# Five rows' weighted sums moved from VectorE to ScalarE and TensorE in a recommender kernel

## The chip, the cores and the metric

The kernel runs on one core of a Trainium2 chip. The metric is the device time of one execution in microseconds (us). TensorE is called PE here, VectorE DVE, ScalarE ACT, GpSimd POOL and SyncE SP, as the profile has them.

## The reference

For each of 512 users there are 200 history rows of 128 numbers, a mask, an age and a popularity per row. The output is one normalised row of 128 numbers per user:

```python
mean_hist = (hist_items * maskf[..., None]).sum(1) / (maskf.sum(1) + 1e-06)
q = mean_hist @ Wq.T
scores = einsum('bd,btd->bt', q, hist_items @ Wk.T) * scale + log(decay + 1e-12)
attn = softmax(where(mask, scores, -inf))
long_term = einsum('bt,btd->bd', attn, hist_items @ Wv.T)
# short_term: mean of up to five rows, those at positions cnt-5 .. cnt-1 (cnt = number of masked rows)
g = sigmoid([mean_pop, mean_rec] @ gate_w.T + gate_b)
user = g * short_term + (1 - g) * long_term
out = (user - mean(user)) / sqrt(var(user) + 1e-05) * ln_gamma + ln_beta
```

The change concerns `g * short_term`, a weighted sum of five rows for each user, and the place of the last three lines.

## The kernel before, in words

A **tile** is 16 users: 128 partitions, 8 for each user, with 25 rows of 128 fp32 numbers in each (1600 KB). There are 32 tiles (0 to 31), two to a pair, and eight tiles (128 users) to a **group**; there are four groups. The output is made group by group.

Every engine has its own program, written out by hand; waits on semaphores tie them together, and each engine takes its instructions strictly in order. PE, ACT and POOL run over **slots** n = 0, 1, 2 ...; slot n is where tile n comes in. With n = 8g + i, `g` and `i` are the group and the place in it. DVE runs over **steps** s = 4g + k of a pair each; step s works on tile 2s-1 and then on tile 2s.

In slot n (for n over 7):

- SP has queued the load of tile n into one of ten buffers; it waits until the tile ten before it has been used up.
- PE makes the masked sums of tile n (`sum_rows`, L457, 25 matmuls), every fourth slot folds earlier results (L508), in slots with i = 7 turns them (L518), makes the attention-weighted sums of tile n-6 (`sum_row_pairs`, L465 and L469, 13 matmuls), the query of tile n-1 (`make_query`, L490) and the mean of tile n (L481). In slots with i = 7 `make_long` (L557) follows, the product of a group's attention sums with Wv, g being one more than that group's number counted from 0.
- ACT copies the weighted sums of tile n-7 (L645) and the mean of tile n-1 (L651), sums the last four of the eight products rows of tile n-3 (`sum_products`, L626, a copy with an accumulator), in odd slots takes two exponentials (L671), copies the masked sums of tile n (L636, with a scale from a tensor), sums the first four products rows of tile n-2 (L626), and copies the query of tile n-1 (L660).
- POOL builds two blocks of weights (`pblk` L345, `mblk` L334) in turns, and multiplies eight rows of tile n-1 by its query (`products`, L357). In a slot with i = 6 it issues the gather of a group's five rows a user into `taken` (L403); at i = 0 `inverse_deviation` (L364).
- DVE takes the dot products of the other 17 rows of each tile with the query, one instruction a row (`dots`, L969; tile 31 has 21), and mixes the rest of its work between them: five steps for the maxima of each pair (`user_maxima`), and a group's finish.

A group's **finish** on DVE is: five weighted rows summed into `short` (`short_term`, L886 and L889, between the dots of tile 8g+3), `finish_scales` in tile 8g+4, then in tile 8g+6 `finish_user` (L988, which waits for `make_long`), `finish_stats`, `finish_moments`, `finish_variance` and `finish_centre` (L1007); `finish_scale` (L1013) is in tile 8g+7. The last group is finished after the last tile's dots. What a slot's work on ACT, PE and POOL waits for is in the functions below.

## Time and profile before

| | |
|---|---|
| device time, median of 3 runs | 175.87 us (175.72 to 178.6) |
| profiled execution | 176.9 us, its span 175.1 us |
| mean granted PE clock | 0.985 |
| busy: PE / DVE / ACT / POOL | 147.1 / 153.0 / 122.2 / 143.8 us |
| DMA, mean over the span | 317 GB/s |

The span runs from the first to the last instruction; the device time has 1.8 us around it. Busy is the time in which an engine worked on an instruction. Instructions of one engine can overlap, and for PE the ends are modelled, so starts are the surer reading. In rows of the timeline the first number is the start in us from the span's start, the second the duration in us; in brackets stands idle time of the engine before it, and what ended it.

### The profile page before, as it was taken

What the parts mean: (1) busy time and instruction counts of PE and PEld (TensorE: products, weight loads), DVE (VectorE), ACT (ScalarE), POOL (GpSimd) and SP (SyncE); (2) the same over time, 40 slices, a digit from 0 to 9 for tenths busy, and PEclk for the clock granted to TensorE, in tenths of its full rate; (3) what the DMA queues carried; (4) which work ended last, traced back from release to release, by engine and by line L of the source; (5) the groups of instructions that cost most, each with busy time, mean ns of one, the idle gap of its engine ahead of it and who ended that gap; (6) DMA issues with size and microseconds to landing.
All of it is one profiled execution on the core that took longest, in us unless ns stands there. A gap on an engine that the chain in (4) does not pass through costs nothing. (4 is left out here: it accounts for less than half of the span.)

```text
span 175.1 us, 8178 instructions
## 1 busy us (share of the span) xinstructions
PE 147.1 (84%) x2811; PEld 113.6 (65%) x2811; DVE 153.0 (87%) x1289; ACT 122.2 (70%) x714; POOL 143.8 (82%) x110
## 2 busy tenths in 40 slices
PE   5766558777679999999998998999998999696780
PEld 5745446666465777877776775877785887364550
DVE  4589849797387899999999999999999999999843
ACT  2021657775385989897988889887889898877420
POOL 5748869889996998999999999999999996975101
PEclk9999996999999999999999999999999999999997
DMA  4799999999999989999999999999999940200000
GB/s 102 269 414 416 253 411 405 406 398 405 416 429 412 362 324 393 408 428 430 407 413 422 416 398 407 413 400 399 415 427 409 371 168 9 50 32 0 19 0 15
DMA packets 8008, 55.48 MB, mean 317 GB/s; under 512 B 2080, under 2 KB 3360, under 8 KB 4000
## 3 DMA queue, kind: packets, MB, share of 16 engines
q1 hardware_dynamic: 7152, 53.59, 77.2%
q0 software_dynamic: 576, 1.33, 2.3%
q8 instruction: 22, 0.36, 0.8%
q14 instruction: 18, 0.15, 0.2%
q10 hardware_dynamic: 240, 0.05, 0.2%
HBM read 54.70 MB, written 0.26 MB: 314 GB/s over the span
## 5 line engine op out<-in xcount | busy, mean ns | idle before, releaser
L969 DVE SCALAR_TENSOR_TENSOR junk_v<-x,ps_query 128x128 f32<-128x128 f32 x548 | 122.0, 279 | 9.6 <-ACT query L660 9.5
L626 ACT ACTIVATE gprod<-gprod 128x128 f32<-128x128 f32 x252 | 74.4, 302 | 11.7 <-POOL gprod L357 11.4
L357 POOL TENSOR_TENSOR gprod<-x,query 128x1024 f32<-128x1024 f32 (+1 forms) x32 | 75.0, 2343 | 8.5 <-ACT query L660 6.0
L457 PE MATMUL ps_acc<-x,mblk 128*16 128x128 f32 x1600 | 56.7, 278 | 6.7 <-DMA x<-in_r_hist_items_dram 6.1
L465 PE MATMUL ps_acc<-x,pblk 128*32 128x256 f32 x768 | 51.6, 381 | 7.9 <-POOL pblk L345 4.8
L457 PEld LDWEIGHTS ps_acc<-x,mblk 128*16 128x16 f32 x1600 | 45.9, 98 | 10.2 <-issue 7.3
L626 ACT ACTIVATION_READ_ACCUMULATOR gprod<-gprod 128x1 f32 x252 | 48.6, 193 | 0.0
L969 DVE DVE_READ_ACCUMULATOR junk_v<-x,ps_query 128x1 f32 x548 | 45.0, 82 | 0.0
L465 PEld LDWEIGHTS ps_acc<-x,pblk 128*32 128x32 f32 x768 | 27.0, 109 | 20.9 <-issue 5.6
L345 POOL TENSOR_TENSOR pblk<-own,ex 128x800 f32<-128x800 f32 (+1 forms) x17 | 24.3, 1432 | 3.8 <-ACT ex L671 3.7
L334 POOL TENSOR_TENSOR mblk<-own,mask_f 128x800 f32<-128x800 f32 (+1 forms) x17 | 25.0, 1471 | 0.2
L636 ACT ACTIVATE sums<-ps_acc,rcnt_rows 128x128 f32<-128x128 f32 x32 | 11.4, 357 | 10.4 <-PE ps_acc L457 10.4
L490 PE MATMUL ps_query<-wqk,mean_p 128*128 128x128 f32 x64 | 15.6, 326 | 2.6 <-ACT mean_p L651 2.6
L490 PEld LDWEIGHTS ps_query<-wqk,mean_p 128*128 128x128 f32 x64 | 9.5, 188 | 9.0 <-issue 5.7
L645 ACT ACTIVATE wx<-ps_acc 128x256 f32<-128x256 f32 x32 | 11.6, 369 | 4.7 <-PE ps_acc L469 3.1
L481 PEld LDWEIGHTS ps_acc<-fold_z,sums 128*128 128x128 f32 x64 | 9.6, 190 | 7.7 <-ACT sums L636 6.6
L481 PE MATMUL ps_acc<-fold_z,sums 128*128 128x16 f32 x64 | 11.0, 248 | 4.0 <-ACT sums L636 3.7
L476 PE MATMUL ps_group<-own_rows 128*128 128x128 f32 x74 | 11.5, 314 | 1.8 <-POOL own_rows L370 1.8
L651 ACT ACTIVATE mean_p<-ps_acc 128x128 f32<-128x128 f32 x32 | 8.8, 274 | 5.2 <-PE ps_acc L481 5.2
L469 PE MATMUL ps_acc<-x,pblk 128*16 128x128 f32 x64 | 12.2, 273 | 0.0
L671 ACT ACTIVATE ex<-kept,nmax_p 128x25 f32<-128x25 f32 x32 | 9.8, 311 | 3.3 <-DVE nmax_p L934 3.3
L476 PEld LDWEIGHTS ps_group<-own_rows 128*128 128x128 f32 x74 | 10.8, 229 | 1.8 <-POOL own_rows L370 1.8
(117 smaller groups left out, 134.0 us busy)
## 6 DMA issues: line engine op xcount, KB each, us to landing
x<-in_r_hist_items_dram SPq DMA_DIRECT2D x31, 1600.0 KB, 10.3
x<-in_r_hist_items_dram SPq DMA_DIRECT2D x1, 832.0 KB, 7.9
x<-in_r_hist_items_dram SPq DMA_DIRECT2D x1, 768.0 KB, 6.3
decay_s<-in_r_hist_age_hours_dram SPq DMA_DIRECT2D x4, 100.0 KB, 13.8
out_dram<-y SPq DMA_DIRECT2D x4, 64.0 KB, 5.0
mask_u<-in_r_hist_mask_dram SPq DMA_DIRECT2D x1, 100.0 KB, 7.1
wq<-in_L_rec_Wq_dram SPq DMA_DIRECT2D x1, 64.0 KB, 7.3
wk<-in_L_rec_Wk_dram SPq DMA_DIRECT2D x1, 64.0 KB, 7.4
```

The lines of the kernel that those rows point to most:

```text
L334: nc.gpsimd.tensor_tensor(mblk[:, s % 2, t:t + tiles, :, :].rearrange("p t r u -> p (t r) u"), own[:, :].unsqueeze(1).broadcast_to([P, til ...
L345: nc.gpsimd.tensor_tensor(pblk[:, s % 2, t:t + tiles, :, :].rearrange("p t r u -> p (t r) u"), own[:, :].unsqueeze(1).broadcast_to([P, til ...
L357: nc.gpsimd.tensor_tensor(gprod[:, t, 0:k * D].rearrange("p (r d) -> p r d", d=D), rows(at(s, t), ROWS - k, ROWS), query[:, s % 2, t, :].u ...
L457: ins = nc.tensor.matmul(dst[c:c + TU, 0:D], blk[:, s % 2, t, m, :], x[:, at(s, t), m * D:(m + 1) * D], start=(m < CG), stop=(m >= ROWS - CG))
L465: nc.tensor.matmul(dst[c:c + 2 * TU, 0:2 * D], blk[:, s % 2, t, m:m + 2, :].rearrange("p r u -> p (r u)"), x[:, at(s, t), m * D:(m + 2) * ...
L469: return nc.tensor.matmul(dst[c:c + TU, 0:D], blk[:, s % 2, t, m, :], x[:, at(s, t), m * D:(m + 1) * D], start=False, stop=True)
L476: nc.tensor.matmul(dst, turned, turned, start=True, stop=True)
L481: nc.tensor.matmul(mean_cols(s, t), sums[:, t, :], fold, start=True, stop=True).then_inc(mean_done, 1)
L490: nc.tensor.matmul(c_query[t], mean_p[:, t, :, :].rearrange("p u c -> p (u c)"), wqk[:, :], start=True, stop=True).then_inc(query_done, 1)
L626: ins = nc.scalar.activation(src, src, ACT.Copy, accum_out=score[:, s % 2, t, at_row:at_row + 1])
L645: nc.scalar.activation(wx[:, s % 2, t, :], wx_bank(s, t)[:, 0:2 * D], ACT.Copy).then_inc(wx_copied, 1)
L969: ins = V.scalar_tensor_tensor(out=junk_v[:, t, r, :], in0=x[:, at(s, t), r * D:(r + 1) * D], scalar=1.0, in1=c_query[t], op0=ALU.mult, op ...
```

## The change

`short_term` goes. ACT now multiplies each gathered row in place by its weight (`scale_taken`: two rows in slots with i = 4, two with i = 5, one with i = 6, and all five of the last group in slot 32). PE adds the five by matmuls with the identity matrix (`make_short`, five matmuls of 128x128, in slots with i = 7 and in slot 33), and ACT copies the sum to `short` (`copy_short`, in slots with i = 0 and in slot 34). `taken` gets two buffers. `make_long` goes from the slot with i = 7 to the next one (the last group's stays), and waits for `copy_short`. DVE's `finish_user` to `finish_variance` go from rows 2 to 5 of tile 8g+6 to rows 11 to 14 of it, `finish_centre` from row 14 of that tile to row 1 of the next, and `finish_scale` from row 1 of that next tile to row 14. `inverse_deviation` goes behind the products in POOL's slot. Of the six matmuls that `keep_busy` issues before the weighted sums of tile 28, two are left.

```diff
+TAKEN_PARTS = {4: (0, 2), 5: (2, 4), 6: (4, LAST)}
-BUSY_FIRST, BUSY_LEAD, BUSY_LAST = 13, 4, {NTILE - 4: 6}
+BUSY_FIRST, BUSY_LEAD, BUSY_LAST = 13, 4, {NTILE - 4: 2}
...
-        taken = sb("taken", [P, LAST, D])
+        taken = sb("taken", [P, 2, LAST, D])
...
             def gather(g):
-                if has(g, 1):
-                    pool.wait_ge(short_part, g * LAST)
+                if has(g, 2):
+                    pool.wait_ge(short_done, g - 1)
...
+            def make_short(q):
+
+                pe.wait_ge(taken_scaled, (q + 1) * LAST)
+                if has(q, 1):
+                    pe.wait_ge(user_ready, q)
+                for i in range(LAST):
+                    ins = nc.tensor.matmul(short_v, ident[:, :], taken[:, q % 2, i, :], start=(i == 0), stop=(i == LAST - 1))
+                ins.then_inc(short_done, 1)
+
             def make_long(g):
+                pe.wait_ge(short_copied, g)
+                pe.wait_ge(rden_ready, g)
                 pe.wait_ge(att_t_ready, g)
-                pe.wait_ge(rden_ready, g)
...
+                if n == NTILE + 1:
+                    make_short(NGROUP - 1)
                 if w == LAST_TILE:
                     sum_weights(g)
...
-                if i == 7 and 0 < g:
+                if i == 0 and 1 < g <= NGROUP:
+                    make_long(g - 1)
+                if i == 7 and 0 < g < NGROUP:
+                    pe.wait_ge(rden_ready, g)
+                    make_short(g - 1)
+                if n == NTILE + 7:
                     make_long(g)
...
+            def scale_taken(q, a, b):
+
+                if a == 0:
+                    act.wait_ge(gathered, q * 16 + 16)
+                    act.wait_ge(gate_ready, 1)
+                for i in range(a, b):
+                    row = taken[:, q % 2, i, :]
+                    nc.scalar.activation(row, row, ACT.Copy, scale=lw[:, bass.ds(q, 1), i]).then_inc(taken_scaled, 1)
+
+            def copy_short(q):
+
+                act.wait_ge(short_done, q + 1)
+                if has(q, 1):
+                    act.wait_ge(user_ready, q)
+                nc.scalar.activation(short[:, :], short_v, ACT.Copy).then_inc(short_copied, 1)
...
+                if n > SLOTS_OF_GROUP and n % SLOTS_OF_GROUP == 0 and n <= NTILE:
+                    copy_short(n // SLOTS_OF_GROUP - 2)
...
+                g, i = divmod(n, SLOTS_OF_GROUP)
+                if 0 < g < NGROUP and i in TAKEN_PARTS:
+                    scale_taken(g - 1, *TAKEN_PARTS[i])
+                if n == NTILE:
+                    scale_taken(NGROUP - 1, 0, LAST)
                 if n == NTILE + 1:
                     copy_weighted(w + 1)
...
-                    if i == (1 if g < NGROUP else DOTS - 3) and k == 0 and has(g, 2, NGROUP):
+                    if i == 1 and k == 0 and has(g, 2, NGROUP):
+                        finish_centre(g - 1)
+                    if i == (DOTS - 3 if g < NGROUP else DOTS_LAST - 2) and k == 0 and has(g, 2, NGROUP):
                         finish_scale(g - 1)
...
-                    if 2 < i < 3 + LAST and k == 2 and fin and has(s, 0):
-                        short_term(g - 1, i - 3)
...
-                    parts = {2: finish_user, 3: finish_stats, 4: finish_moments, 5: finish_variance, 14: finish_centre}
+                    parts = {11: finish_user, 12: finish_stats, 13: finish_moments, 14: finish_variance}
                     if g == NGROUP:
-                        parts[15] = finish_scale
+                        parts.update({15: finish_centre, 16: finish_scale})
```

PE, slots 23 and 24 (the second group's), before: L490 is the query, L481 the mean, L557 `make_long`, L457 the masked sums, L465 and L469 the weighted sums.

```order
L490 MATMUL ps_query<-wqk,mean_p 128x128
L481 MATMUL ps_acc<-fold_z,sums 128x16
L557 MATMUL ps_fin<-wv_t,att_t 128x128
L457 MATMUL ps_acc<-x,mblk 16x128 x25
L465 MATMUL ps_acc<-x,pblk 32x256 x12
L469 MATMUL ps_acc<-x,pblk 16x128
L490 MATMUL ps_query<-wqk,mean_p 128x128
L481 MATMUL ps_acc<-fold_z,sums 128x16
L457 MATMUL ps_acc<-x,mblk 16x128 x25
```

The same place now (every line number is one higher up to L491; L562 is `make_short`, L570 `make_long`):

```order
L491 MATMUL ps_query<-wqk,mean_p 128x128
L482 MATMUL ps_acc<-fold_z,sums 128x16
L562 MATMUL ps_fin<-taken,ident 128x128 x5
L458 MATMUL ps_acc<-x,mblk 16x128 x25
L466 MATMUL ps_acc<-x,pblk 32x256 x12
L470 MATMUL ps_acc<-x,pblk 16x128
L491 MATMUL ps_query<-wqk,mean_p 128x128
L482 MATMUL ps_acc<-fold_z,sums 128x16
L570 MATMUL ps_fin<-wv_t,att_t 128x128
L458 MATMUL ps_acc<-x,mblk 16x128 x25
```

Five matmuls stand where `make_long` stood, and `make_long` stands one slot, that is 40 other matmuls, later.

ACT, slot 21 (i = 5), before: four products rows of tile 18, two exponentials, the masked sums of tile 21, four products rows of tile 19, the query of tile 20.

```order
L626 ACTIVATE gprod,score<-gprod 128x128 x4
L671 ACTIVATE ex,wsum<-kept,nmax_p 128x25 x2
L636 ACTIVATE sums<-ps_acc,rcnt_rows 128x128
L626 ACTIVATE gprod,score<-gprod 128x128 x4
L660 ACTIVATE query<-ps_query 128x128
```

Now:

```order
L646 ACTIVATE gprod,score<-gprod 128x128 x4
L691 ACTIVATE ex,wsum<-kept,nmax_p 128x25 x2
L656 ACTIVATE sums<-ps_acc,rcnt_rows 128x128
L710 ACTIVATE taken<-taken,lw 128x128 x2
L646 ACTIVATE gprod,score<-gprod 128x128 x4
L680 ACTIVATE query<-ps_query 128x128
```

Two scaled copies of gathered rows stand ahead of the products rows and of the query.

DVE, the second half of tile 22 (its rows 9 to 16) and the first rows of tile 23, now; L1001 is a dot, L1019 `finish_user`, L1024 to L1033 the three steps behind it, L1038 `finish_centre`, L966 the last of the five steps for a pair's maxima:

```order
L1001 SCALAR_TENSOR_TENSOR junk_v,score<-x,ps_query 128x128
L1019 SCALAR_TENSOR_TENSOR ps_dve<-ps_fin,long_scale,short 128x128
L1001 SCALAR_TENSOR_TENSOR junk_v,score<-x,ps_query 128x128
L953 STREAM_TRANSPOSE pmax_t<-pmax 128x32
L1024 BN_STATS bn<-ps_dve 128x6
...
L1033 TENSOR_SCALAR vare<-mv 128x1
L1001 SCALAR_TENSOR_TENSOR junk_v,score<-x,ps_query 128x128 x2
L966 STREAM_TRANSPOSE nmax_p<-numax 128x32
L1001 SCALAR_TENSOR_TENSOR junk_v,score<-x,ps_query 128x128 x2
L1038 SCALAR_TENSOR_TENSOR ps_dve<-ps_dve,mv,gam 128x128
```

`finish_user` stood behind two dots of this tile; now eleven dots and two of the maxima's steps are ahead of it.

## Rows read from the trace of the kernel before

**Rows 1.** Busy time of each engine in a stretch; last PE clock, DMA share, GB/s.
```profile
110.00:120.00 10.00, 10.00 (x232) 8.17 (x235) 9.96 (x97) 8.80 (x56) 9.56 (x7) 1.00 1.00 401
```

**Rows 2.** Timeline of DVE, tile 27: two of the five rows' steps, a dot between.
```profile
142.22 0.35 DVE L889 SCALAR_TENSOR_TENSOR ps_dve<-taken,lw,ps_dve 128x128 f32<-128x128 f32 x1
142.48 0.28 DVE L969 SCALAR_TENSOR_TENSOR junk_v<-x,ps_query 128x128 f32<-128x128 f32 x1
...
142.68 0.35 DVE L889 SCALAR_TENSOR_TENSOR ps_dve<-taken,lw,ps_dve 128x128 f32<-128x128 f32 x1
```

**Rows 3.** Timeline of POOL, products of tiles 20 to 23.
```profile
110.38 2.38 POOL L357 TENSOR_TENSOR gprod<-x,query 128x1024 f32<-128x1024 f32 x1
...
114.37 2.37 POOL L357 TENSOR_TENSOR gprod<-x,query 128x1024 f32<-128x1024 f32 x1
116.91 1.02 POOL L403 DMA_INDIRECT taken<-in_r_hist_items_dram,first_row  x1 [0.17 <-issue]
...
119.47 2.40 POOL L357 TENSOR_TENSOR gprod<-x,query 128x1024 f32<-128x1024 f32 x1
...
124.05 2.36 POOL L357 TENSOR_TENSOR gprod<-x,query 128x1024 f32<-128x1024 f32 x1
```

**Rows 4.** Timeline of ACT, slots 21 and 22.
```profile
108.37 0.35 ACT L636 ACTIVATE sums<-ps_acc,rcnt_rows 128x128 f32<-128x128 f32 x1
108.83 0.31 ACT L626 ACTIVATE gprod<-gprod 128x128 f32<-128x128 f32 x1
...
112.86 0.31 ACT L626 ACTIVATE gprod<-gprod 128x128 f32<-128x128 f32 x1 [0.70 <-POOL gprod L357]
...
114.04 0.25 ACT L660 ACTIVATE query<-ps_query 128x128 f32<-128x128 f32 x1
```

**Rows 5.** Groups of instructions of ACT and PE by form: busy us, mean ns.
```profile
L636 ACT ACTIVATE sums<-ps_acc,rcnt_rows 128x128 f32<-128x128 f32 x32 | 11.4, 357 | 10.4 <-PE ps_acc L457 10.4
L660 ACT ACTIVATE query<-ps_query 128x128 f32<-128x128 f32 x32 | 8.4, 261 | 4.0 <-PE ps_query L490 4.0
...
L476 PE MATMUL ps_acc<-own_rows 128*128 128x128 f32 x12 | 1.6, 284 | 0.0
```

**Rows 6.** Timeline of PE: queries of tiles 17 and 23, `make_long` between them.
```profile
97.51 0.49 PE L490 MATMUL ps_query<-wqk,mean_p 128*128 128x128 f32 x2
...
118.31 0.47 PE L557 MATMUL ps_fin<-wv_t,att_t 128*128 128x128 f32 x2
...
121.85 0.49 PE L490 MATMUL ps_query<-wqk,mean_p 128*128 128x128 f32 x2
```

**Rows 7.** Timeline of ACT, the copy of tile 17's query.
```profile
98.04 0.28 ACT L660 ACTIVATE query<-ps_query 128x128 f32<-128x128 f32 x1
```

**Rows 8.** Timeline of DVE: tile 22's `finish_user` and row 11, tile 23's first row.
```profile
120.57 0.35 DVE L988 SCALAR_TENSOR_TENSOR ps_dve<-ps_fin,long_scale,short 128x128 f32<-128x128 f32 x1
...
123.30 0.28 DVE L969 SCALAR_TENSOR_TENSOR junk_v<-x,ps_query 128x128 f32<-128x128 f32 x1
...
125.08 0.29 DVE L969 SCALAR_TENSOR_TENSOR junk_v<-x,ps_query 128x128 f32<-128x128 f32 x1
```

**Rows 9.** Timeline, the end: PE's and ACT's slot 32, tile 31's first dot.
```profile
154.88 0.49 PE L490 MATMUL ps_query<-wqk,mean_p 128*128 128x128 f32 x2
...
155.55 0.31 ACT L626 ACTIVATE gprod<-gprod 128x128 f32<-128x128 f32 x1 [1.29 <-POOL gprod L357]
...
156.73 0.25 ACT L660 ACTIVATE query<-ps_query 128x128 f32<-128x128 f32 x1
...
158.75 0.28 DVE L969 SCALAR_TENSOR_TENSOR junk_v<-x,ps_query 128x128 f32<-128x128 f32 x1
...
166.32 1.50 PE L465 MATMUL ps_acc<-x,pblk 128*32 128x256 f32 x24 [1.07 <-DVE pblk L954]
```

**Rows 10.** The last gather alone (its line, 148 to 156 us).
```profile
L403 POOL DMA_INDIRECT taken<-in_r_hist_items_dram,first_row x1: 1022/1022/1022, 150.5 to 150.5; - x1
...
DMA to landing us min/median/max: 3.8/3.8/3.8
```

More of the change, by code:

```diff
@@ L164, in build @@
         hide_v, at = ps_dve[:, 0:GROUP_ROWS], GROUP_ROWS
-        short_v, user_v = ps_dve[:, at:at + D], ps_dve[:, at + D:at + 2 * D]
+        user_v, short_v = ps_dve[:, at + D:at + 2 * D], ps_fin[:, 384:384 + D]
         own_v, rden_v = ps_dve[:, at + 2 * D:at + 2 * D + TU], ps_dve[:, at + 2 * D + TU:at + 2 * D + TU + 1]
@@ L185, in build @@
         gate_in, gate_exp, gate_ready, rows_ready = sem("gate_in"), sem("gate_exp"), sem("gate_ready"), sem("rows_ready")
-        short_part = sem("short_part")
+        taken_scaled, short_done, short_copied = sem("taken_scaled"), sem("short_done"), sem("short_copied")
         gathered = sem("gathered")
@@ L399, in gather @@
             def gather(g):
[L401 to L402 removed]
+                if has(g, 2):
+                    pool.wait_ge(short_done, g - 1)
                 nc.gpsimd.indirect_dma_start(
[L404 removed]
+                    out=taken[:, g % 2, :, :].rearrange("p i d -> p (i d)"), out_offset=None, in_=items_rows,
                     in_offset=bass.IndirectOffsetOnAxis(ap=first_row[:, g:g + 1], axis=0)).then_inc(gathered, 16)
@@ L413, in slot @@
                     build_pblk(w)
-                if i == 0 and has(g, 2, NGROUP):
-                    inverse_deviation(g - 2)
                 if tile(n + 2) and n % PAIR == 0:
@@ L426, in slot @@
                     build_pblk(FIRST_LONE + 1, 1)
+                if i == 0 and has(g, 2, NGROUP):
+                    inverse_deviation(g - 2)
                 if n < NGROUP:
@@ L547, in sum_weights @@
                 pe.wait_ge(wsum_ready, g)
+                if g == NGROUP:
+                    pe.wait_ge(short_copied, g)
                 if g == 1:
@@ L723, in slot @@
                 if n == NTILE + 2:
+                    copy_short(NGROUP - 1)
                     sum_products(LAST_TILE, 0, ROWS - DOTS_LAST)
@@ L879, in setup_last_weights @@
                 dve.wait_ge(gate_ready, 1)
-            def short_term(g, i):
-                w = lw[:, bass.ds(g, 1), i]
-                if i == 0:
-                    dve.wait_ge(gathered, g * 16 + 16)
-                    ins = V.tensor_scalar(short_v, taken[:, i, :], w, None, ALU.mult)
-                else:
-                    dve.wait_ge(short_part, g * LAST + i)
-                    ins = V.scalar_tensor_tensor(out=short_v if i < LAST - 1 else short[:, :], in0=taken[:, i, :], scalar=w,
-                                                 in1=short_v, op0=ALU.mult, op1=ALU.add)
-                ins.then_inc(short_part, 1)
             def group_hide(g):
@@ L1053, in step @@
                                 last_block()
-                                for j in range(LAST):
-                                    if j == LAST - 2:
-                                        lay_out_sums(s + 1)
-                                    short_term(g - 1, j)
+                                lay_out_sums(s + 1)
                     if i in parts:
```

3 lines of the change are left out of this document (1 added, 2 removed).

## The prediction

> **What bounds the kernel now.** I read the windows first, then the timeline of each engine in one group of slots, then the end. The window shows DVE at 9.96 of 10 us, PE at 10.00, POOL at 9.56, ACT at 8.80 and the DMA share at 1.00 [rows 1]. Five things are near full, so the busiest cannot be named from shares; the reader has to look for who waits for whom.
>
> POOL's products give the pace. Those of tile 20 start at 110.38 and those of tile 21 at 114.37, 3.99 us later; the next two starts, with a gather and the reciprocal root between them, are at 119.47 and 124.05 [rows 3]. The 3.99 is a loop: products of 2.38, after which ACT, idle for them [0.70 at 112.86], sums four rows and copies the next query at 114.04, for 0.25, and POOL starts at 114.37 [rows 3, 4]. DVE has no part in this loop. From tile 21 to 22 POOL alone sets the time: its gather starts at 116.91 and the weights' block follows it up to 119.47 [rows 3].
>
> DVE is full, but it runs behind the queries: tile 31's query is ready at 156.73 + 0.25 = 156.98, and its first dot is at 158.75, 1.77 us later [rows 9]. So a shorter DVE programme first eats that backlog, and then DVE waits for queries. At the very end DVE does set the time: PE waits for DVE's last block until 166.32 [rows 9], and all that follows hangs on it. What counts is thus when tile 31's dots begin, and how many steps lie among them.
>
> **The change, part by part.** The sum is for tile 31's first dot and what is behind it.
>
> Removed: five steps a group on DVE. One step starts at 142.22, a dot at 142.48, the next step at 142.68: a step takes 0.26 and a dot 0.20 of DVE's time [rows 2]. Three groups have theirs in the full stretch: 15 x 0.26 = 3.9 us. The last group's five come after the last dots, beside PE's last weighted sums and ahead of nothing that ends late; I cost them at nothing. They can at most give 1.3 if that cover were not there.
>
> Added on ACT: a row's scaled copy. The trace has no such copy from SBUF with a scale from a tensor. The plain copy from PSUM takes 261 ns, the one with such a scale 357 ns [rows 5], so 0.10 is the scale; a products row takes 0.31 from SBUF [rows 4]. A lone copy would be some 0.40, and neighbours overlap; I take 0.30 a row, with ends at 0.20 and 0.40. In slots with i = 4 and 6 ACT has 0.70 idle before the products rows, as at 112.86 [rows 4], which covers two copies or one. With i = 5 it hasn't: in slot 21 the masked sums end at 108.37 + 0.35 = 108.72 and the products row starts at 108.83 [rows 4], 0.11 of room for 0.60. These copies stand in the loop, ahead of the query, so 0.49 goes into the pace, once a group (slots 13, 21, 29): 3 x 0.49 = 1.5 us (0.9 to 2.1). In slot 32 all five stand before products rows that start at 155.55 after 1.29 idle [rows 9]: 1.5 - 1.29 = 0.2 (0 to 0.7). They wait for the last gather too, issued at 150.5 and landed 3.8 later, at 154.3 [rows 10], just when that idle time begins (154.26); if it came 1 us later, the query of tile 31 would, and what hides it is only that the loads have ended by then. `copy_short` has the 0.25 of a query's copy [rows 4] and lies in slots whose idle time covers it; if not, 0.25 a group.
>
> Added on PE: `make_short`. Six matmuls of 128x128 in a row take 1.6 us [rows 5], so five take 1.33 and are 1.33 late for all that PE does after them: masked sums, weighted sums, queries. What hides that is PE's lead over ACT. It isn't everywhere: PE's query of tile 17 ends at 97.51 + 0.49 = 98.00, ACT copies it at 98.04 [rows 6, 7], a lead of 0.04. ACT's own delay of 0.49 covers a part. Ends: nothing (the lead elsewhere is larger and PE catches up) and 1.33 - 0.49 = 0.84 in each of three groups. I take 0.1 a group, 0.3 in all, nearer to the low end, since the end of the stretch has room: PE's last `make_short` in a busy slot stands before weighted sums that wait for POOL.
>
> The new wait on DVE: `finish_user`, now in row 11 of tile 8g+6, waits for `make_long`, now a slot later and behind `make_short`. In the second group the query before it starts at 121.85 [rows 6]; with 1.33 added and `make_long`'s own share (its 0.47 [rows 6], 0.4 of it between neighbours) gone, that is 122.8; it takes 0.49, `make_long` 0.47: done at 123.75. DVE's row 11 began at 123.30 with four steps of the finish ahead of it [rows 8], which now stand behind it. At some 0.15 each (0 to 0.26) that is 122.7, and with the 1.3 saved 121.4. So DVE waits 1.0 to 2.3 us, and all dots behind it and the pair's maxima wait too, which ACT's exponentials need. From row 11 to the next tile are 125.08 - 123.30 = 1.78 [rows 8], plus 0.6 for the four steps, less 0.2 for `finish_centre`, moved on: 2.2. Tile 23 starts at 125.95 and not 125.08: the saved 1.3 is gone, and 0.9 more. It is DVE's backlog that takes this up, since the next group saves another 1.3 before its own wait.
>
> At the end the same: PE's query of tile 31 ends at 154.88 + 0.49 [rows 9], `make_long` at 155.85, row 11 of tile 30 then, and tile 31 starts 2.2 later at 158.05, not 158.75: a gain of 0.7, whatever DVE saved earlier. Of the moves, `finish_centre` is now among tile 31's dots: 0.25 back. `inverse_deviation` stays in POOL's queue, behind one products instruction, and the sum of POOL's work is the same: nothing. A `gather` waits for `short_done` of two groups before, long done: nothing.
>
> `keep_busy` loses four matmuls in the gap before tile 28's weighted sums, and `make_short` puts five into it: nothing, at a granted clock of 1.00 [rows 1]. If the clock did fall there, a weighted sum of 1.50 [rows 9] would take up to 1.5 more.
>
> **Sum.** Delay of the queries: 1.5 + 0.2 + 0.3 = 2.0. Gain at tile 31: 0.7 - 0.25 = 0.45. Net 1.5 us later. The profiled execution took 176.9 us with a span of 175.1, so 178.4; it was 1.03 above the median of 175.87, so the median is forecast at 177.4. The range of this case by the bounds: 176.0 to 179.3.
>
> **Rivals.** *A, the backlog goes and little else.* The copies overlap better than I think or slot 21 has more room, and `make_long` comes in time for DVE. Then tile 31 starts when its query is ready: 1.77 earlier [rows 9], less 0.25 for `finish_centre`: 1.5 faster, 174.4. For it speaks that ACT idles in two slots of three; against it the 0.11 us in slot 21 and the 121.85 of PE's query.
>
> *B, PE is the pacemaker.* PE shows 10.00 of 10 us busy [rows 1] and a lead of 0.04 at tile 17. If it has no time to catch up, each group adds the full 1.33 of `make_short`: 4.0, + 0.2 - 0.45 = 3.75 us, 179.6. It decides from the point where PE's lead over ACT stays under 1.33 through a whole group. Against it: PE's ends are modelled, so its busy share is too high.
>
> *C, the fullest engine sets the time.* If DVE bounds the stretch, as 9.96 of 10 suggests, all 3.9 us come back: 172.0. Against it is the lag of the dots behind the queries, which DVE cannot make shorter for POOL. The Trainium skill (Perfetto Trace Analysis, Identifying the Most-Contended Engine) says that the engine with the highest occupancy is the one to relieve first, and by that rule this rival would be the forecast; the lag of 1.77 us speaks against it here.
>
> **Chances.** Forecast 0.56, A 0.26, B 0.13, C 0.05. A measurement of this kernel tells about 2%, 3.5 us, from no change: faster by over that is C alone, 0.05; slower by over that (from 179.4) is most of B and the forecast's upper end, 0.12; within it 0.83. The range holds 8 in 10: it takes in the forecast, most of A (down to 174.0) and the nearer half of B (179.9).
>
> **What would show each step.** ACT: the products row of slot 21 starts some 0.5 late after the two scaled copies, each with a duration near 0.40; the idle time in slots 20 and 22 shrinks by 0.6 and 0.3. DVE: before `finish_user` in tiles 14, 22 and 30 a wait of 1 to 2 us that ends with `make_long`; DVE's share falls below 9.7 of 10. POOL: products of tile 8g+5 half a microsecond later in each group, so that eight tiles take over 34 us. PE: five matmuls in 1.3 us. Tile 31's first dot near 160.0. I am wrong if the scaled copies are hidden (A), if PE's queries come later than ACT is free (B), or if the last gather lands late enough to hold ACT in slot 32.

## The result and the profile after

| | before | changed |
|---|---|---|
| device time, median of 4 runs | 175.84 us (175.72 to 178.6) | 180.24 us (179.7 to 180.71) |
| profiled execution, its span | 176.9, 175.1 us | 179.7, 178.0 us |
| mean granted PE clock in it | 0.985 | 0.978 |

The medians lie 4.4 us apart. The ratio, which takes only executions within 1.5% of a kernel's fastest, is 1.0225 with a 95% interval of 1.0175 to 1.0276: 3.1 to 4.8 us slower, and whether by more than 2% isn't settled. The forecast was 177.4, and its range ended at 179.9. By the ratio the change stands at 175.87 x 1.0225 = 179.8, just inside; its own median, 180.24, is just outside. The direction was right and the size too small.

The profiled executions lie only 2.8 us apart, and 0.7 of that is there before any of the moved work runs. So I read one stretch: from tile 10's first dot to the start of the last `y`, the kernel's last computation. Its rows on DVE in the changed kernel (start, duration) are tile 10's first dot, tile 31's first dot and the last `y`:

```profile
70.44 0.29 DVE L1001 SCALAR_TENSOR_TENSOR junk_v<-x,ps_query 128x128 f32<-128x128 f32 x1
...
161.26 0.28 DVE L1001 SCALAR_TENSOR_TENSOR junk_v<-x,ps_query 128x128 f32<-128x128 f32 x1
...
175.66 0.35 DVE L1044 SCALAR_TENSOR_TENSOR y<-ps_dve,rstd,bet 128x128 f32<-128x128 f32 x1 [0.40 <-POOL rstd L365]
```

The same of before; its dot between is in [rows 9]:

```profile
69.75 0.29 DVE L969 SCALAR_TENSOR_TENSOR junk_v<-x,ps_query 128x128 f32<-128x128 f32 x1
...
172.81 0.35 DVE L1013 SCALAR_TENSOR_TENSOR y<-ps_dve,rstd,bet 128x128 f32<-128x128 f32 x1 [0.40 <-POOL rstd L364]
```

Before takes 172.81 - 69.75 = 103.06 us, 89.00 of it up to tile 31's first dot. The changed kernel takes 175.66 - 70.44 = 105.22, with 90.82 up to that dot: 2.16 us more. The rest of the 2.8, 0.69, lies ahead of tile 10.

What the forecast named is in the profile. ACT, slots 21 and 22, where [rows 4] had the masked sums, a pause of 0.11 and the products row:

```profile
111.03 0.35 ACT L656 ACTIVATE sums<-ps_acc,rcnt_rows 128x128 f32<-128x128 f32 x1
111.28 0.69 ACT L710 ACTIVATE taken<-taken,lw 128x128 f32<-128x128 f32 x2
111.87 0.30 ACT L646 ACTIVATE gprod<-gprod 128x128 f32<-128x128 f32 x1
...
113.03 0.27 ACT L680 ACTIVATE query<-ps_query 128x128 f32<-128x128 f32 x1
```

Two copies take 0.59 from the first one's start to the products row's, so 0.30 each, as taken. ACT in slot 32 has the last group's five, and it waited 0.49 for the last gather there, the risk that the forecast named. Then DVE's waits from 80 to 172 us (total, times, longest):

```profile
157.72 1.57 ACT L710 ACTIVATE taken<-taken,lw 128x128 f32<-128x128 f32 x5 [0.49 <-DMA taken<-in_r_hist_items_dram,first_row]
```
```profile
DVE ps_dve L1019 <- PE ps_fin L570: 4.8, 3, 2.2
```

`finish_user` now waits for `make_long` three times, 2.22, 1.83 and 0.77 us, as the forecast had it for the first two (1.0 to 2.3). Less of DVE's time is busy too: 9.60 of 10 us from 110 to 120, 8.02 from 120 to 130.

These waits give an account of the stretch from DVE's side. In the kernel before DVE waits for nothing between the first dots of tiles 10 and 31, so those 89.00 us are the length of its own programme. The changed one is 3.9 us of steps shorter, has `finish_centre` (0.25) more, and waits 4.8 for `make_long` and 0.4 for a query: 89.00 - 3.65 + 5.2 = 90.55, and 90.82 was measured. At the end the chain is the forecast's, one matmul behind the other (PE, then DVE):

```profile
158.36 0.49 PE L491 MATMUL ps_query<-wqk,mean_p 128*128 128x128 f32 x2
158.68 0.39 PE L570 MATMUL ps_fin<-wv_t,att_t 128*128 128x128 f32 x2
```
```profile
159.11 0.36 DVE L1019 SCALAR_TENSOR_TENSOR ps_dve<-ps_fin,long_scale,short 128x128 f32<-128x128 f32 x1 [0.77 <-PE ps_fin L570]
```

Tile 31's first dot comes 2.15 us after this `finish_user` (forecast 2.2). So what has to be explained is why PE's query of tile 31 is late: it starts 87.92 us after tile 10's first dot, and 85.13 before [rows 9], 2.8 later. A place where it enters is on PE and on what follows it, slots 17 and 18 (PE, ACT, POOL):

```profile
98.41 0.38 PE L509 MATMUL ps_group<-wx,fold_odd_z 128*32 128x128 f32 x2 [1.94 <-issue]
...
100.14 0.49 PE L491 MATMUL ps_query<-wqk,mean_p 128*128 128x128 f32 x2
```
```profile
100.66 0.28 ACT L680 ACTIVATE query<-ps_query 128x128 f32<-128x128 f32 x1 [1.49 <-PE ps_query L491]
```
```profile
101.02 2.39 POOL L358 TENSOR_TENSOR gprod<-x,query 128x1024 f32<-128x1024 f32 x1 [1.71 <-ACT query L680]
```

PE stands still for 1.94 us in the middle of the folds of weighted sums, on nothing that the profile names; then its query of tile 17 is late, ACT waits 1.49 for it and POOL 1.71. In the kernel before, the same place had a stall of its own, "[0.88 <-issue]" at 96.34, and PE's query came 0.04 ahead of ACT [rows 6, 7].

POOL's products need the queries, so their starts show where the queries become late. How much later they start than before, each kernel counted from its own tile 10, in us (negative is earlier; worked out from the starts of POOL's products):

| tile | 12 | 16 | 17 | 20 | 24 | 28 | 31 |
|---|---|---|---|---|---|---|---|
| before, again (e0) | 0.01 | 0.47 | 0.43 | 0.41 | 0.23 | 0.45 | 0.47 |
| changed | 0.49 | 0.38 | 1.93 | 2.30 | 2.15 | 2.76 | 2.95 |
| changed, again | 0.50 | 0.38 | 1.54 | 1.89 | 1.72 | 2.84 | 2.90 |
| e1, PE's part | 0.46 | 1.38 | 1.35 | 1.33 | 1.20 | 1.63 | 1.65 |
| e2, ACT's part | 1.37 | 1.64 | 1.81 | 2.20 | 2.04 | 2.43 | 2.74 |
| e3, DVE's relief | -0.01 | 0.17 | 0.44 | 0.46 | 0.49 | 1.04 | 1.06 |
| e9, fewer matmuls | 0.99 | 1.08 | 1.06 | 1.95 | 1.80 | 2.57 | 3.18 |
| e12, all moved | 0.70 | 0.84 | 0.81 | 0.87 | 0.75 | 0.82 | 0.83 |

The row of the unchanged kernel is the measure of noise here: up to 0.6 us (0.59 at tile 13), of which nothing reached DVE's dots, since they run at least 0.9 behind their queries. Tile 31's first dot came after 89.01 us in it, against 89.00. In the changed kernel three steps stand where ACT's copies do: 0.49 by tile 12, 0.34 at tile 20, 0.36 at tile 28. One step, 1.55 at tile 17 (1.16 in the second execution), stands behind the stall of PE.

### The profile page after: what moved, and what is told of

Its sections match the earlier page's. It is cut to its first block and busy times, and to the rows that moved or that the text cites. A ratio compares the mean times of both kernels' runs of the same rounds, so it can differ in the third digit from the quotient of the medians.

```text
span 178.0 us, 8258 instructions
## 1 busy us (share of the span) xinstructions
PE 149.9 (84%) x2843; PEld 117.4 (66%) x2843; DVE 148.2 (83%) x1269; ACT 128.4 (72%) x738; POOL 143.9 (81%) x110
## 3 DMA queue, kind: packets, MB, share of 16 engines
q0 software_dynamic: 576, 1.33, 2.2%
## 5 line engine op out<-in xcount | busy, mean ns | idle before, releaser
L1001 DVE SCALAR_TENSOR_TENSOR junk_v<-x,ps_query 128x128 f32<-128x128 f32 x548 | 121.1, 281 | 10.8 <-ACT query L680 10.5
L458 PE MATMUL ps_acc<-x,mblk 128*16 128x128 f32 x1600 | 58.1, 282 | 7.0 <-DMA x<-in_r_hist_items_dram 5.0
L458 PEld LDWEIGHTS ps_acc<-x,mblk 128*16 128x16 f32 x1600 | 46.7, 99 | 11.2 <-issue 7.5
L646 ACT ACTIVATION_READ_ACCUMULATOR gprod<-gprod 128x1 f32 x252 | 49.6, 197 | 0.0
L1001 DVE DVE_READ_ACCUMULATOR junk_v<-x,ps_query 128x1 f32 x548 | 45.7, 83 | 0.0
L466 PEld LDWEIGHTS ps_acc<-x,pblk 128*32 128x32 f32 x768 | 27.6, 109 | 17.2 <-issue 5.0
L491 PE MATMUL ps_query<-wqk,mean_p 128*128 128x128 f32 x64 | 15.6, 326 | 3.1 <-ACT mean_p L671 2.6
L491 PEld LDWEIGHTS ps_query<-wqk,mean_p 128*128 128x128 f32 x64 | 9.5, 188 | 9.2 <-issue 5.9
L680 ACT ACTIVATE query<-ps_query 128x128 f32<-128x128 f32 x32 | 8.5, 267 | 5.5 <-PE ps_query L491 5.5
```

Source lines behind the costliest of these rows:

```text
L458: ins = nc.tensor.matmul(dst[c:c + TU, 0:D], blk[:, s % 2, t, m, :], x[:, at(s, t), m * D:(m + 1) * D], start=(m < CG), stop=(m >= ROWS - CG))
L466: nc.tensor.matmul(dst[c:c + 2 * TU, 0:2 * D], blk[:, s % 2, t, m:m + 2, :].rearrange("p r u -> p (r u)"), x[:, at(s, t), m * D:(m + 2) * ...
L491: nc.tensor.matmul(c_query[t], mean_p[:, t, :, :].rearrange("p u c -> p (u c)"), wqk[:, :], start=True, stop=True).then_inc(query_done, 1)
L646: ins = nc.scalar.activation(src, src, ACT.Copy, accum_out=score[:, s % 2, t, at_row:at_row + 1])
L1001: ins = V.scalar_tensor_tensor(out=junk_v[:, t, r, :], in0=x[:, at(s, t), r * D:(r + 1) * D], scalar=1.0, in1=c_query[t], op0=ALU.mult, op ...
```

## The experiments

Whole times of the kernel before spread from 175.7 to 184.8 us over the chips that these runs fell on; in the profiled executions up to 5 us of that lie ahead of tile 10 (69.75 and 74.91). "Stretch" is always tile 10's first dot to the last `y`, "lag" is tile 31's first dot minus the end of ACT's copy of its query (1.77 before, 0.63 after). The stretch repeated to 0.1 us in the two executions of each of the two kernels. Each experiment's is from one execution, though, and the traces show that this isn't always enough: several differ from their kernel before their edit has had any effect. Where that is so, it is said.

**e0 and e7: both kernels once more,** unchanged, on another chip, the same for both.

> The kernel before, unchanged, for one profile beside the others of this chip. From the first dot of tile 10 to the first dot of tile 31 it took 89.0 us in the first profile (69.75 to 158.75); 88.7 to 89.6 is expected again, whatever the start of the execution costs.

> The changed kernel, unchanged, again beside the kernel before on one chip. It was 4.4 us slower (1.0225); the forecast had 1.5. If the forecast's terms are right and the rest was the chip's start, 1 to 2.5 us slower; if the full price is real, 3 to 5. From tile 10's first dot to tile 31's the first profile of it took 90.8 us.

The kernel before, execution of 182.05 us:

```profile
74.91 0.29 DVE L969 SCALAR_TENSOR_TENSOR junk_v<-x,ps_query 128x128 f32<-128x128 f32 x1
...
177.98 0.35 DVE L1013 SCALAR_TENSOR_TENSOR y<-ps_dve,rstd,bet 128x128 f32<-128x128 f32 x1 [0.39 <-POOL rstd L364]
```

The changed kernel, execution of 182.99 us:

```profile
73.69 0.29 DVE L1001 SCALAR_TENSOR_TENSOR junk_v<-x,ps_query 128x128 f32<-128x128 f32 x1
...
178.95 0.35 DVE L1044 SCALAR_TENSOR_TENSOR y<-ps_dve,rstd,bet 128x128 f32<-128x128 f32 x1 [0.40 <-POOL rstd L365]
```

103.07 and 105.26: the stretch's 2.2 us stand. Ahead of tile 10 the order has turned, 74.91 for the kernel before and 73.69 for the changed one, so the 0.69 of the first pair is within what executions differ by. The medians of this chip are 183.81 (6 runs) against 181.71 (11 runs), 2.1 apart; the fastest runs are further apart (181.87 against 176.93 and 177.27), so whole times leave the size open.

**e1: PE's part alone,** on the kernel before: five matmuls of 128x128 into an idle bank, read by nobody, at the end of slots 15 and 23, ahead of the masked sums of tiles 16 and 24.

```diff
+                if n > SLOTS_OF_GROUP and n % SLOTS_OF_GROUP == 0:
+                    keep_busy(sum_bank(s, t)[:, 3 * D:4 * D], LAST)
```

> The kernel before, with five matmuls of 128x128 added on PE where make_short now stands (slots 15, 23, 31, ahead of the next masked sums), and nothing else; they write an unused part of a bank, the output is the reference's. Theory ACT (the forecast: PE has lead enough to take most of it): 0 to 0.8 us slower. Theory PE (PE is the pacemaker, rival B): 1.33 us a group for two or three groups, 2.5 to 4 us slower.

Stretch 104.39, 1.3 longer, but this is not the price of the ten matmuls. The first of them starts at 92.34. Tile 13's products had started at 88.05, already 1.49 later than before, and tile 14's first dot came 1.04 later; PE had stopped on the way, among instructions that both kernels have:

```profile
84.90 0.50 PE L457 MATMUL ps_acc<-x,mblk 128*16 128x128 f32 x9 [1.14 <-issue]
```

Behind the added matmuls the products are no later: 1.49 at tile 14, 1.35 at tile 17, 1.20 at tile 24. At tiles 16 and 24, right behind them, the steps are 0.01 and 0.02. So here ten matmuls cost the queries nothing that can be seen, and rival B's 1.33 a group is not there. What five matmuls cost where PE's lead is 0.04, this run can't say, since it ran late anyway. The median was 181.74 against 182.44 (ratio 1.0066, 0.990 to 1.023): whole times can't resolve it.

**e2: ACT's part alone,** on the kernel before: the scaled copies go to a spare tile, from the identity matrix, in the changed kernel's slots.

```diff
+                for i in range(a, b):
+                    nc.scalar.activation(spare[:, i, :], ident[:, :], ACT.Copy, scale=lw[:, bass.ds(q, 1), i])
```

> The kernel before, with scaled copies added on ACT where scale_taken now stands (two in slots 8g+4, two in 8g+5, one in 8g+6, five in slot 32); they copy the identity matrix with a weight as scale into a spare tile, the output is the reference's. Theory ACT: 0.49 us a group, 1.5 us and up to 0.2 for slot 32, so 1.5 to 1.7 us slower. Theory PE (ACT has room, PE sets the pace): 0 to 0.5 us slower.

Stretch 105.06, 2.0 longer, median 181.87 (6 runs) against 182.44. Not all of it is the copies' either: PE, unchanged, stopped for 0.54 and 0.86 us in slots 12 and 14, and the products were 1.01 late at tile 11, where the changed kernel's were 0.13. The steps that stand at the copies are 0.36 at tile 12, 0.35 at tile 20, 0.38 at tile 28 and 0.31 at tile 31, 1.4 in all, and the same places and nearly the same sizes as in the changed kernel. This is what shows ACT's part. Since e1 and e2 each carry such a delay, their 1.3 and 2.0 can't be added or compared with the 2.2.

**e3: DVE's relief alone,** on the kernel before: of a group's five scaled rows it computes only the last.

```diff
-                if i == 0:
-                    ins = V.tensor_scalar(short_v, taken[:, i, :], w, None, ALU.mult)
-                else:
...
+                if i == LAST - 1:
+                    V.tensor_scalar(short[:, :], taken[:, i, :], w, None, ALU.mult).then_inc(short_part, 1)
```

> The kernel before, with one of the five steps of short_term on DVE left (the fifth row times its weight alone; the other four rows are left out of the output). It prices the relief of DVE: 4 x 0.26 = 1.04 us a group. Theory backlog (DVE runs behind the queries and its relief is worth at most the lag of tile 31's dots): 1.0 to 1.8 us faster. Rival C (the fullest engine bounds the stretch): 3.1 us faster. If relief is worth nothing: within 0.3.

Stretch 102.85, 0.2 us shorter (whole times 181.62 against 182.44, ratio 0.984, 0.976 to 0.993). The relief was smaller than planned, though. The step that was left now writes to SBUF at once, and instead of 0.26 it took 1.53, 0.28 and 0.92 us in the three groups. The long ones end with an instruction of POOL, at 81.58 and 81.50 the first time (DVE, then POOL):

```profile
80.05 1.53 DVE L886 TENSOR_SCALAR short<-taken,lw 128x128 f32<-128x128 f32 x1
```
```profile
79.95 1.55 POOL L345 TENSOR_TENSOR pblk<-own,ex 128x800 f32<-128x800 f32 x1
```

So DVE won some 1.4 us (3.9 less 2.5) and not 3.1. Its dots were 0.93 earlier at tile 22; then they waited for queries (0.7 us in all), which in this execution ran up to 1.06 later than before, behind stalls of PE. The lag fell from 1.77 to 0.24 and 0.46 was left at tile 31. DVE's own programme did set the time of the kernel before up to there, as its missing waits show; what its relief can win is bounded by how far its dots lie behind the queries, at least 0.93 and at most 2.4 us. The 3.9 of rival C aren't there to be had, but this run alone doesn't show it; e12 does.

**e4: `make_long` back in its slot,** on the changed kernel, so that DVE needn't wait for it.

```diff
-                if i == 0 and 1 < g <= NGROUP:
-                    make_long(g - 1)
                 if i == 7 and 0 < g < NGROUP:
-                    pe.wait_ge(rden_ready, g)
+                    make_long(g)
                     make_short(g - 1)
```

> The changed kernel, with make_long back in the slot with i = 7, ahead of make_short, and without its wait for copy_short (finish_user waits for copy_short instead). If the 1 to 2.3 us for which DVE waits at finish_user in tiles 14, 22 and 30 cost the end, this takes them away: 0.5 to 2 us faster than the changed kernel's 180.2, so 178.2 to 179.7. If PE or ACT set the pace, DVE's wait only eats its backlog: within 0.5 of the changed kernel.

DVE's waits for `make_long` are gone but for the one at the very end (the 4.8 us of the three full groups), and in their place it waits 6.0 us for queries. The stretch is 106.62, 1.4 longer than the changed kernel's. The products start 4.54 later at tile 31, 2.71 of it by tile 17. But tile 14's first dot, ahead of the first instruction that differs, was already 2.0 us later than in the changed kernel (PE had stopped for 1.14 us in slot 14), and from there on this run is 0.6 us shorter. The whole times point that way too: median 182.42 (8 runs) against 182.44 for the kernel before on that chip, ratio 0.989 (0.977 to 1.000), where the changed kernel's was 1.0225. Whether `make_long`'s old place wins something stays open.

**e6: one matmul where `make_short` has five,** on the changed kernel; the sum is the last row alone.

```diff
-                for i in range(LAST):
-                    ins = nc.tensor.matmul(short_v, ident[:, :], taken[:, q % 2, i, :], start=(i == 0), stop=(i == LAST - 1))
+                for i in range(LAST - 1, LAST):
+                    ins = nc.tensor.matmul(short_v, ident[:, :], taken[:, q % 2, i, :], start=True, stop=True)
```

> The changed kernel with one of make_short's five matmuls left (the fifth row's; the sum of the other four is left out of the output). Theory PE: 4 x 0.27 = 1.07 us a group come back, 2 to 3.2 us faster than the changed kernel. Theory ACT (the scaled copies in slots 13, 21 and 29 and DVE's wait are the price): within 0.8 of it, and faster mostly by what DVE waits less for make_long.

Less work on PE, and the stretch is 108.21, 3.0 longer (median 184.58, 6 runs, against 183.81 for the changed kernel and 181.71 for the kernel before on that chip). This is no effect of the edit in the main: `make_short` first runs at 91.8, and tile 14's first dot, ahead of it, was already 2.3 us later than in the changed kernel. What differs is PE's rows with idle time that no wait explains:

```profile
84.14 0.50 PE L458 MATMUL ps_acc<-x,mblk 128*16 128x128 f32 x9 [1.88 <-issue]
...
104.40 1.27 PE L466 MATMUL ps_acc<-x,pblk 128*32 128x256 f32 x17 [2.27 <-issue]
...
143.29 0.40 PE L458 MATMUL ps_acc<-x,mblk 128*16 128x128 f32 x4 [1.53 <-issue]
```

They stand in the middle of rows of equal matmuls, one after another from one tile. Taking every idle time of PE's weight loads over 0.42 us that no wait explains and that follows a transfer on the queue of instructions, there are 11.1 us of such stalls in the stretch, against 6.7 in the changed kernel and 3.3 before, 6.1 in e0. Each follows a transfer on the queue of instructions: one lands at 82.63, 103.02 and 141.83, and PE goes on 1.4 to 1.5 us later. In the changed kernel, from 96.05 to 97.1 us (packets, MB, share):

```profile
q8 instruction: 1, 0.02, 5.5%
```

That packet of 16 KB starts at 96.11 and takes 0.93; PE, stopped since 96.5, goes on at 98.41, 1.4 us after it landed. At the 21 such places in the stretches of four kernels (before, changed, e6, e8) the distance is 1.3 to 1.5.

The places are fixed by the count of instructions. Counting PE's weight loads from the start of the program, they come ahead of the 1101st, 1226th, 1351st, 1477th, 1603rd, 1728th, 1853rd, 1978th, 2103rd, 2229th, 2354th or 2480th, one off at most, in e0 and e1 too: 125 or 126 apart or a multiple of that, whatever stands there. Their length isn't fixed. Ahead of the 1101st, which stands ahead of what the edits change on PE in these kernels, the gap between two weight loads was 0.40 before, 1.21 in e0, 1.51 in e1, 0.31 in the changed kernel and 2.26 in e6. So a change that adds or removes matmuls moves work against these points, and how long PE stands at each differs from one execution to the next.

**e8: the changed kernel with its programme shifted** by sixteen one-column matmuls in slots 2 to 5, ahead of everything measured.

```diff
+                if 2 <= n <= 5:
+                    for _ in range(4):
+                        nc.tensor.matmul(ps_group[:, D:D + 1], ident[:, :], ones[:, :], start=True, stop=True)
```

> The changed kernel with 16 one-column matmuls added on PE in slots 2 to 5, where PE waits for loads: they cost nothing there, and shift by 64 instructions where the loads of PE's own instructions fall in the program. From tile 10's first dot to the last y the changed kernel took 105.2 and 105.3 us, with PE stalled in slot 18 for 2.2 to 2.3 us with nothing that it waited for. Theory supply (these stalls are PE waiting for instructions, and it is they that make PE late): the stalls move to other places and the stretch changes by 0.5 to 2 us, either way. Theory work (PE is late by make_short's 1.33 us a group alone): the stalls move and the stretch stays at 105.2 within 0.3.

```profile
111.53 0.85 PE L458 MATMUL ps_acc<-x,mblk 128*16 128x128 f32 x24 [1.14 <-issue]
...
117.73 1.27 PE L466 MATMUL ps_acc<-x,pblk 128*32 128x256 f32 x18 [0.99 <-issue]
```

The stall that ends at 111.53 belongs to the one transfer that took long, 107.58 + 2.50 = 110.08: again 1.45 after the landing, and not after the start. These two stand ahead of the 1728th and the 1854th weight load again, which is now work of 32 weight loads earlier. The stall in front of tile 17's query is gone, and so is the step there (0.65 late at tile 17, not 1.93), although `make_short` is as it was; other steps came at tiles 20 and 21 instead (1.53, then 2.28), and the stretch is 105.65 (median 183.34, 4 runs, against 180.65 for the kernel before on that chip). So the step at tile 17 needs the stall, and this shift won nothing by moving it.

**e9 and e10: both kernels with a quarter fewer matmuls.** The masked sums take two rows per matmul (128x256), and two matmuls of the mean fold them. PE's count of matmul instructions (two for each matmul of the program) falls from 2843 to 2139 in the changed kernel and from 2811 to 2107 in the kernel before, the transfers of instructions from 22 to 17.

```diff
-                sum_rows(sum_bank(s, t), mblk, s, t, 0, loaded).then_inc(sum_done, 1)
+                for a, part_loaded, count in loaded[:1]:
+                    pe.wait_ge(part_loaded, count)
+                sum_row_pairs(sum_bank(s, t), mblk, s, t, 0, loaded[1:]).then_inc(sum_done, 1)
```

> The changed kernel with the masked sums made like the weighted ones, by row pairs of 256 columns (13 matmuls in place of 25 a tile, one more matmul for each mean, ACT copies 256 columns and not 128; the output is the reference's). PE's busy time of a tile hardly changes (1.9 us for 1.7), its instructions of a slot fall by about a quarter. Theory supply: stalls without a wait nearly vanish, PE leads ACT everywhere but by its work, and the stretch from tile 10's first dot to the last y is 1 to 2 us shorter than 105.2. Theory work: 0.1 us a slot more on ACT and 0.2 on PE, so 1 to 3 us longer.

> The kernel before with the same row pairs for the masked sums (the output is the reference's). Its stretch from tile 10's first dot to the last y was 103.07 in two executions, with 3.7 and 6.5 us of such stalls, so PE has enough lead there. Theory supply and theory ACT agree: no gain in that stretch, 0 to 2 us longer for ACT's wider copy (0.1 us a slot) in the odd slots. A gain of over 0.5 would say that PE sets the pace before the change too.

In e9, PE's waits from 70 to 176 us name engines alone, the longest of them POOL, while the changed kernel's begin with two that name none (1.9 and 1.6 us):

```profile
PE ps_acc L469 <- POOL pblk L346: 1.6, 2, 1.1
```

Without a stall the stretches are 105.19 and 103.05, within 0.1 of the 105.22 and 103.06 with them (medians 181.29 and 180.97, 4 runs each, too few to tell 2 us in the whole time). So the stalls don't make the 2.2 us between the kernels: the change costs 2.1 in a pair that has none. This pair is the cleanest in the document. In e9 the step at tile 17 is gone (1.08 at 16, 1.06 at 17), and the steps at ACT's copies are larger, 0.99 at tile 12, 0.89 between tiles 17 and 20, 0.77 between 24 and 28; ACT's masked sums are wider here too, so how much of that is the copies alone isn't shown. Up to tile 31's first dot POOL waits 6.4 us for ACT's query in e9 and 2.0 in e10; ACT waits for no query of PE in e9. And DVE, which waits for nothing in e10 until then, has these waits in e9 from 70 to 162 us:

```profile
DVE ps_dve L1025 <- PE ps_fin L576: 4.7, 3, 2.3
DVE junk_v L1007 <- ACT query L686: 0.8, 2, 0.5
```

By DVE's account, 5.5 of waits less 3.65 of relief are 1.85, and tile 31's first dot is 1.80 later than in e10. So without stalls it is ACT that holds the queries up, and DVE loses by waiting more than it won by working less.

**e5: ACT's copies in even slots,** where it idles for POOL (i = 2, 4, 6), for two of the three groups.

```diff
+TAKEN_EVEN = {2: (0, 2), 4: (2, 4), 6: (4, LAST)}
...
-                if 0 < g < NGROUP and i in TAKEN_PARTS:
-                    scale_taken(g - 1, *TAKEN_PARTS[i])
+                parts = TAKEN_PARTS if g == 1 else TAKEN_EVEN
+                if 0 < g < NGROUP and i in parts:
+                    scale_taken(g - 1, *parts[i])
```

> The changed kernel with the scaled copies of the second and third group in slots with i = 2, 4 and 6, where ACT has idle time, and none in i = 5 (the first group's must stay). Theory ACT: 2 x 0.49 = 1.0 us faster than the changed kernel. Theory PE: within 0.3 of it.

The step between tiles 24 and 28 shrank from 0.61 to 0.43, and at tile 28 itself from 0.36 to 0.01, as the theory of ACT has it; yet at tile 20, with the first such group, it was 1.2 from tile 17, not 0.37, with a stall of PE of 2.25 us on the way (0.93 in the changed kernel). The stretch is 105.59, 0.4 worse than the changed kernel's, with stalls of 7.5; the median is 182.65 (6 runs), 1.2 better than the changed kernel's 183.81 on that chip. So the copies' price in slots with i = 5 went at tile 28, and what the whole gains stays open.

**e12: all of it at once:** e4's order, e5's slots, e9's pairs, and in slot 32 three copies before tile 31's query and two behind it.

```diff
-                    scale_taken(NGROUP - 1, 0, LAST)
+                    scale_taken(NGROUP - 1, 0, 3)
...
+                if n == NTILE:
+                    scale_taken(NGROUP - 1, 3, LAST)
```

> The changed kernel with every cost that the runs point to moved off: masked sums by row pairs (no PE stalls), make_long back in the slot with i = 7 (no wait on DVE in tiles 14, 22 and 30), the scaled copies of groups 2 and 3 in slots with i = 2, 4, 6, those of group 1 as two, one and two, and of the last group's five only three ahead of tile 31's query. If the relief of DVE is worth its 1.77 us of lag once nothing else is late: the stretch from tile 10's first dot to the last y is 101.6 to 102.6, against 103.07 of the kernel before. If ACT's copies and PE's five matmuls cost wherever they stand: 103.5 to 105.5. Rival C (DVE bounds): 99.5 to 100.5.

```profile
74.53 0.29 DVE L1008 SCALAR_TENSOR_TENSOR junk_v<-x,ps_query 128x128 f32<-128x128 f32 x1
...
162.81 0.29 DVE L1008 SCALAR_TENSOR_TENSOR junk_v<-x,ps_query 128x128 f32<-128x128 f32 x1
...
164.56 0.18 DVE L947 TENSOR_TENSOR kept<-score,ps_dve 128x25 f32<-128x25 f32 x1 [0.57 <-ACT gprod L650]
...
177.97 0.35 DVE L1052 SCALAR_TENSOR_TENSOR y<-ps_dve,rstd,bet 128x128 f32<-128x128 f32 x1 [0.40 <-POOL rstd L366]
```

Now the queries are only 0.83 late at tile 31 and the lag is 0.03: tile 31's dots begin after 88.28 us, 0.7 earlier than before. But all of DVE's relief, 3.65 us, has bought no more than that: it has caught up and waits for queries nine times, 2.4 us in all. This is what shows that rival C's 3.9 aren't to be had. From tile 31's first dot, 1.75 us later, it waits 0.57 for ACT's rows of an earlier tile. From that dot to the last `y` are 15.16 us, not 14.06. The stretch is 103.44: 1.8 better than the changed kernel, and no better than the kernel before (103.06). The whole times say more, 179.11 (6 runs) against 180.51 (11 runs), ratio 0.981 (0.974 to 0.989): faster, by 2% or not. That gain lies ahead of tile 10 or in what executions differ by, and no run here says which.

## Why the prediction was right or wrong

Its sum was a delay of the queries, less what tile 31's dots win on them, plus what is added behind. Each has its number, for the first profiled pair:

| term | forecast | measured |
|---|---|---|
| ACT's copies in three groups | 3 x 0.49 = 1.5 | 0.49 + 0.34 + 0.36 = 1.2 |
| slot 32 | 0.2 | 0.18 |
| PE's `make_short` | 0.3 | 1.55, at tile 17 (1.16 in e7) |
| all that delays tile 31's products | 2.0 | 2.95 |
| lag of tile 31's dots | -0.7 | 0.63 - 1.77 = -1.14 |
| behind the first dot | 0.25 | 14.40 - 14.06 = 0.34 |
| sum | 1.5 | 2.2 |

**ACT: right.** Durations, place and cover are as written; two of three groups cost 0.35 instead of 0.49, in the changed kernel and in e2. The Trainium skill (ScalarE: Activation LUTs, What ACT_TABLE_LOAD costs) gives for an ACTIVATE 186 ns plus 0.833 ns an element, 93 ns for a scale from a tensor and an overlap of 93 between neighbours. An estimate from these figures is 0.29 us for a row of 128. The trace agrees, 0.30.

**DVE's new wait: right in size and in the chain at the end,** 2.2, 1.8 and 0.8 us, with tile 31's first dot 2.15 behind `finish_user`. But it isn't hidden by a backlog, as the forecast had it for the groups ahead: with the 0.4 for a query it is more than the 3.65 that DVE saved, and its first dots are 1.2 later than before already at tile 16. Without it the queries bound DVE (e4, e12).

**PE: the step that failed.** The forecast took 0.1 a group for `make_short`, where its own upper end was 0.84, and 1.55 (1.16 in e7) was measured at tile 17. The term was off by 1.25, more than the two sums differ (0.7), so part of it was made up elsewhere, by the larger loss of lag and ACT's smaller steps: luck. Two things were wrong in it. The trace had a lead of only 0.04 us at tile 17's query [rows 6, 7], which is no cover for 1.33. And the sum had no term for PE's stalls: one stood at that place before, and grew from 0.88 to 1.94. Where no stall stands at tile 17 the step is gone with `make_short` still there (e8, e9), and from tile 22 to tile 25, with `make_short` in slot 23 between, the products fall no further behind (2.30 to 2.16). So the five matmuls' own work is as small as forecast wherever these runs can see it, and the stall is what was missing. How the added work made the stall longer isn't shown; its transfer starts 1.5 us later from tile 10's first dot than before. The 1.55 isn't to be read as a cost that could be had back by itself either: e9 has no stall, and its stretch is as long.

**The range.** Its bounds don't follow from the terms as written: the low ends add up to 0.9 + 0 + 0 - 0.45, the high ends to 2.1 + 0.7 + 2.5 - 0.45, which is 176.3 to 180.7 and not 176.0 to 179.3. The measured median lies in the wider one.

**Rivals.** A, the backlog alone (174.4), fell with ACT's steps. B, PE as the pacemaker at 1.33 a group, fell with e1, where products behind ten added matmuls are no later, and with e8. C, the fullest engine (172.0), is half right: DVE did set the pace of the stretch, but only up to its lag behind the queries, 0.93 to 2.4 us, and e12 got 0.7 for 3.65. The rule of the Trainium skill (Perfetto Trace Analysis, Identifying the Most-Contended Engine) is to relieve the engine with the highest occupancy first, here DVE with 9.96 of 10 us. The trace agrees that DVE set the pace; how little its relief wins stands in the lag.

**The measured 4.4.** The stretch explains 2.2, in two pairs of executions. Of the profiled pair's other 0.7, e0 and e7 show that its sign can turn. The remaining 1.6 is in the medians alone: before's lies 1.06 below its profiled execution, the changed one's 0.54 above, and the other three runs of the changed kernel took 179.8 to 180.7 at a mean clock of 0.953 to 0.964, against 0.978 in the profiled one. From 20 to 60 us that profiled one already had less clock than the one before (0.92 against 0.96), and PE 0.8 us more busy time (31.25 against 30.46).

Whether the change itself makes that clock lower stays open. Against it speaks that the kernel before had 0.953 over its whole span in e0, and that on e7's chip the medians were 2.1 apart, the stretch's own difference.

`keep_busy` with two matmuls instead of six showed nothing: the granted clock stayed at 1.00 from 110 to 170 us in the changed kernel, as it did before.

## What to carry to other kernels

Where several engines are nearly full, relieving the fullest wins no more than the distance to the next, which is read from who is late for whom and not from shares. Here 3.65 us less on DVE could win 0.7, and the work was moved onto the two engines that feed the queries, with a new wait of DVE on one of them. A lead of a few hundredths of a microsecond covers nothing: cost what is put ahead of it at its full length, once. A difference of 1% is better read between two fixed instructions of the trace than from whole times, but from more than one execution: look first whether the runs already differ ahead of the first instruction that was changed. Three experiments here did, by 1 to 2.3 us. And an experiment that drops work may change what is left of it, as the step in e3 that went to SBUF.

## What was not expected of the hardware

PE stopped in the middle of a row of independent matmuls, its weight loads for up to 2.2 us in the changed kernel, with no wait on any semaphore, and went on 1.3 to 1.5 us after a 16 KB transfer on the queue of instructions had landed (most took 0.9 to 1.1 us beside loads that kept the DMA share at 1.00). There are 22 such transfers for 2843 matmul instructions and as many weight loads, and 17 for 2139, so some 256 instructions each, and the stalls stand 125 or 126 weight loads apart, or a multiple of that. The Trainium skill (Advanced Engine Details and Errata, ISA Cache) gives 16 KB or 256 instructions as one line of the cache of instructions; the counts agree. Sixteen small matmuls more ahead of the stretch moved other work onto these points, and with a quarter fewer instructions the stalls were gone. Their length at one and the same point differed from 0.3 to 2.3 us between executions. That the transfers cause the stalls is inferred from these times: no run held a transfer back.

A step of DVE from SBUF to SBUF, 0.28 us long at two of its four places in e3, took 1.53 and 0.92 us at the others and ended 0.08 us after an instruction of POOL both times (81.58 after 81.50, 148.30 after 148.22). That it waited for POOL is inferred from these ends.
